# Products of probs and values issued in four runs per group of heads instead of ten

## What is computed

```python
xn = layernorm(x)                                   # x: (2, 1024, 512) float32
q, k, v = split(xn @ w_qkv.T + b_qkv)               # 32 heads of 16
scores = q @ k.T / 4 + slope[head] * (key - 1023)   # ALiBi bias, causal mask
s = (softmax(scores) @ v) @ w_out.T + b_out
g = silu(down(silu(gate(xn)) * up(xn)))             # octonion-structured, ternary weights
out = x + s * g
```

## Time and profile before

| | |
|---|---|
| Median of 3 runs | 980.35 us (979.74 to 981.66) |
| Span of the profiled execution, first to last instruction | 976.7 us |
| Median less span | 3.65 us |
| TensorE matmul busy | 920.3 us, 94% |
| VectorE busy | 648.4 us, 66% |
| ScalarE busy | 464.6 us, 48% |
| Mean granted TensorE clock | 0.978 of 2.4 GHz |
| Scores, L1257 and L1262 | 190.4 and 87.2 us of TensorE |
| Products, L1273 | 126.2 us without those that read the reused buffer |
| Maxima, L1244 and L1247 | 208.3 and 86.4 us of TensorE |

### The profile page before, as it was taken

How to read it: one execution, slowest core, us unless ns; L and a number is a source line. 1 busy time by engine, 2 the same in 40 slices (tenths; PEclk the granted TensorE clock), 3 DMA queues, 4 the chain that set the end, 5 groups by cost and what they waited for, 6 DMA issues and landing times.

```text
span 976.7 us, 17352 instructions
## 1 busy us (share of the span) xinstructions
PE 920.3 (94%) x5886; PEld 500.9 (51%) x5886; DVE 648.4 (66%) x1169; ACT 464.6 (48%) x634; POOL 109.8 (11%) x117
## 2 busy tenths in 40 slices
PE   3796999999999987999999999999999999999977
PEld 3672458546845663444444444444444444443565
DVE  5778434544454333855888878788888878883488
ACT  3573532233143211216566666666666566657610
POOL 1121203230322121210000000000000000000032
PEclk9897999999999998999999999999999999999999
DMA  7421004202400239801544676445765446743748
GB/s 202 157 82 60 1 33 154 74 1 100 145 13 11 81 131 130 99 12 44 67 75 75 87 100 89 65 71 75 100 89 75 73 72 89 100 121 109 242 155 325
DMA packets 78170, 92.36 MB, mean 95 GB/s; under 512 B 26829, under 2 KB 43213, under 8 KB 78129
## 3 DMA queue, kind: packets, MB, share of 16 engines
q1 hardware_dynamic: 78017, 91.54, 43.6%
q0 software_dynamic: 112, 0.27, 0.1%
HBM read 57.57 MB, written 33.82 MB: 94 GB/s over the span
## 4 chain that ended last, share of the span: by engine, by line
PE 52%; DMA 4%; DVE 2%; issue 2%; SPq 2%; ACT 1%; DVEq 0%; ACTq 0%
PE psum L1273 14%; PE psum L1244 14%; PE psum L1257 12%; PE psum L1247 3%; PE psum L1262 3%; DMA o_scr<-osum 2%; PE psum L248 2%; PE psum L249 2%; DMA r_scr<-den 1%; DMA probs<-in_L_attn_x 1%; PE psum L259 1%; PE psum L260 1%; DVE mx L1137 1%; SPq L1011 1%; SPq L1016 1%
## 5 line engine op out<-in xcount | busy, mean ns | idle before, releaser
L1137 DVE TENSOR_REDUCE mx<-psum 128x1 f32<-128x512 f32 (+3 forms) x608 | 372.2, 658 | 83.8 <-PE psum L1247 48.2
L1094 ACT ACTIVATE probs<-psum 128x1024 f32<-128x1024 f32 (+1 forms) x256 | 222.8, 915 | 117.6 <-PE psum L1262 97.7
L1244 PE MATMUL psum<-Ks,Qs 99*128 99x512 bf16 (+3 forms) x768 | 208.3, 329 | 7.5 <-issue 5.6
L1257 PE MATMUL psum<-Qs,Ks 102*128 102x512 bf16 (+3 forms) x768 | 190.4, 326 | 2.1 <-DVE g_stage L304 1.6
L248 PE MATMUL psum<-X,MG 128*128 128x512 f16 (+1 forms) x352 | 136.7, 388 | 5.0 <-PEq L322 3.7
L249 PE MATMUL psum<-X,MG 128*128 128x512 f16 (+1 forms) x352 | 136.4, 387 | 0.0
L1244 PEld LDWEIGHTS psum<-Ks,Qs 99*128 99x128 bf16 x768 | 65.6, 98 | 134.7 <-DVE mx L1137 76.9
L1273 PE MATMUL psum<-probs,Vs 128*32 128x512 f32 (+3 forms) x1152 | 126.2, 521 | 0.0
L1257 PEld LDWEIGHTS psum<-Qs,Ks 102*128 102x128 bf16 x768 | 72.0, 98 | 55.6 <-ACT probs L1094 8.4
L276 ACT ACTIVATE hid<-psum,sig_scale 128x512 f32<-128x512 f32 (+1 forms) x44 | 30.2, 687 | 147.5 <-PE psum L249 147.5
L1262 PE MATMUL psum<-identb,causal 128*128 128x128 bf16 (+1 forms) x384 | 87.2, 237 | 0.0
(11 more groups left out here) (124 smaller groups left out, 1093.0 us busy)
## 6 DMA issues: line engine op xcount, KB each, us to landing
Qs<-q_scr SPq DMA_DIRECT2D x96, 128.0 KB
Ks<-k_scr SPq DMA_DIRECT2D x96, 128.0 KB
o_scr<-osum SPq DMA_DIRECT2D x32, 256.0 KB, 4.1
q_scr<-qk_stage SPq DMA_DIRECT2D x16, 384.0 KB, 2.4
k_scr<-qk_stage SPq DMA_DIRECT2D x16, 384.0 KB, 2.5
v_scr<-v_stage SPq DMA_DIRECT2D x16, 256.0 KB, 2.0
g_scr<-g_stage SPq DMA_DIRECT2D x16, 256.0 KB, 2.0
Vs<-v_scr SPq DMA_DIRECT2D x16, 256.0 KB
```

What stands on the lines that cost most here:

```text
L1094: nc.scalar.activation(probs[n % PSLOTS][:, 2 * pair:2 * pair + 2, 0:COLS[n]], s_bank[pair][:, :, 0:COLS[n]], ACT.Exp, scale=1.0 / INV_SCA ...
L1137: nc.vector.tensor_reduce(dst, m_bank[bank][:, 0:n * keys].rearrange("p (n k) -> p n k", n=n), AX.X, ALU.max).then_inc(max_read, 1)
L1244: last = nc.tensor.matmul(tile[:, hh, :], Qs[s][0:ROWS_MAX, h + hh, qb * P:(qb + 1) * P], Ks[s][0:ROWS_MAX, h + hh, k0:k0 + keys], start=( ...
L1257: last = nc.tensor.matmul(bank[:, at:at + cols], Ks[s][0:ROWS_ALL, 2 * pair + h, kb * P:(kb + 1) * P], Qs[s][0:ROWS_ALL, 2 * pair + h, (c ...
```

## The change

A table RUNS says after the scores of which step which products are listed. After step 1: those of steps 7, 8 and 9 of the group before; after step 4: 0, 1 and 2; after step 6: 3 and 4; after step 8: 5 and 6. The costs that interleave gives them are the same, and so are the maxima and their pacing, the matmuls themselves, all semaphores and counts, the exps and their places on ScalarE, and SP's queue. After the last group steps 7, 8 and 9 follow as before.

```diff
--- before.py
+++ after.py
@@ -103,6 +103,7 @@
 LAST_PACE = 0.7
 LAG = 3
 PSLOTS = 5
+RUNS = {1: (-1, (7, 8, 9)), 4: (0, (0, 1, 2)), 6: (0, (3, 4)), 8: (0, (5, 6))}
 LATE = [t % SLOTS for t in (QUADS - 3, QUADS - 2)]
 
 
@@ -121,10 +122,8 @@
     main = []
     for n in range(NST):
         main += [("scores", 0, (n, pair), 2 * COLS[n] + 2 * P * len(STEPS[n][1]) * (n in DIAG)) for pair in range(2)]
-        if n >= LAG:
-            main.append(("products", 0, n - LAG, 4 * COLS[n - LAG]))
-        elif not first:
-            main.append(("products", -1, NST + n - LAG, 4 * COLS[NST + n - LAG]))
+        if n in RUNS and not (first and RUNS[n][0]):
+            main += [("products", RUNS[n][0], m, 4 * COLS[m]) for m in RUNS[n][1]]
     items = [(1, i) for i in range(LEAD, NITEM)] if ahead else []
     items += [(2, i) for i in (range(LEAD) if lead else [ROWS_AT])] if ahead else []
     cost = [PARTS_COST if i == ROWS_AT else MAXT[i - (i > ROWS_AT)][2] * MAXT[i - (i > ROWS_AT)][4] + 64 for _, i in items]
```

## The result

The changed kernel takes 1031.26 us, the median of four runs (1029.92 to 1031.76), against 980.67 us (979.74 to 981.66) of the kernel before in the same rounds: a ratio of 1.052 [1.0505, 1.0536], 5.2% slower. The forecast was 1033.7. Between the medians lie 50.6 us, where the forecast added 53.3; the two profiled executions, each one run out of several, lie 53.2 apart (spans of 1029.9 and 976.7 us).

The account below looks back on a forecast made before the run. TensorE's order was taken to price each group. Adding 1 + 46.5 + 5.8 = 53.3 us for group 0, thirteen groups and the end to 980.35 gave 1033.7 us, 5.4% slower, range 1018 to 1042.

Parts of the forecast that it names:

- Rival A: Runs behave as announced, ScalarE is not in the way and only switches go: 18 us faster, 962 us; chance 0.03.
- rival C: Stalls as forecast but the switches saved too, 2.3 us a group: 1017 us with the ends; chance 0.05.
- ScalarE's cover: Steady groups: scores following each other with only maxima between wait for ScalarE's exps, 3.58 us a group, 46.5 over thirteen.
- rival B: No change: same work, ten switches, and maxima cover ScalarE wholly; 980 us; chance 0.04.
- S2 S3 S4: Scores of steps 2 to 4, up to product 0: TensorE waits for ScalarE's exps and copy, 1.54 us lost a group.
- S5 S6: Scores of steps 5 and 6, up to product 3: TensorE waits for exps, 0.76 us lost a group.
- S7 S8: Scores of steps 7 and 8, up to product 5: TensorE waits for exps, 0.40 us lost a group.
- S9 S0 S1: Scores of steps 9, 0 and 1 over the group's border: TensorE waits for exps, 0.88 us lost a group.
- The ends: Group 0 adds 1 us (0 to 3.6); group 14 and the start of group 15 add 5.8 us.
- The last store: Kernel's end: the last osum waited 3.85 us for SP; group 15 uses 2.5 of it, still covered.
- rival D: Dearer: m5's DMA or the last store comes late on top, 1038 to 1045 us; chance 0.06.
- The switch: TensorE between full-width matmuls and 32-column products: 0.22 us both ways, made as often as before, so 0 saved.

Follow-up runs that it names:

- closed: Changed kernel with maxima kept out of the product runs and put behind them, so TensorE switches four times a group in place of ten: 1043.74 us, ratio 1.0655.
- one_run: Order of the kernel before, ten single product places, except that products 0, 1 and 2 all stand after the scores of step 4: 1003.56 us, ratio 1.0228.
- split_two: Kernel before, with only the products of steps 3 and 5 cut into halves with a maximum between, two more switches a group: 1001.80 us, ratio 1.0209.
- split: Kernel before, with the products of steps 0 and 3 to 7 cut into halves with a maximum between, six more switches a group: 1015.96 us, ratio 1.0366.

## Why the prediction was right

**The order.** The forecast said that maxima stay between the products of a run and that no switch is saved. It was right: in the trace after the change ten separate runs of products stand in a group, so the four of the title are those of the list, not of what is issued, and keeping the maxima out (the kernel with real runs) changed the time by another 12.5 us. Rival A (962) and rival C (1017) rested on adjacency and fall with it; "closed" adds that adjacency alone would not have brought the gain of A either.

**ScalarE's cover.** Shown by the pair with shorter exps: 21 us in the new order, nothing in the old one. That excludes rival B. The waits came where they were forecast, and the longest at step 4 (0.74 us where 0.9 was forecast); a small one at step 0 (0.17) was not named:

| stretch | forecast, us | measured, us |
|---|---|---|
| S2 S3 S4 | 1.54 | 1.49 (one_run: 1.50 as a period) |
| S5 S6 | 0.76 | 0.72 (0.47 + 0.25) |
| S7 S8 | 0.40 | 0.27 |
| S9 S0 S1 | 0.88 | 0.66 (0.17 + 0.14 + 0.35) |
| sum | 3.58 | 3.14 |
| period less before's | 3.58 | 3.35 (33.26 - 29.91) |

The walk priced the stretches of plain scores to 0.05 us and was too dear where masked scores and the group's border lie. Some 0.2 us of the period lie outside these stretches; I can't place them.

**The ends.** Cut at the copies of a group's second half, the 53.2 us between the two profiled executions fall into five parts. The first score came at 448.24 and comes at 449.23: 1.0 us that the change can't have made, within the scatter of that start. From there to group 0's copy (484.55, now 488.42): 2.9 us, where the forecast had 1, with a bound of 3.6 (the copy comes after step 2 of group 1, so a piece of it is group 1's). The thirteen periods from there to group 13's (873.38, now 920.76): 43.5, forecast 46.5. From there to group 14's (900.39, now 953.12): 5.3, forecast 5.8. To the end: 0.5, forecast 0. That the sum agrees to 0.1 us is luck: terms that were too large and too small cancel, single terms are up to 3 us off, and 1.0 us is scatter. Between the medians it is 50.6, 2.7 less than forecast. The largest term, the period, was priced 0.23 us too dear, 3.0 over thirteen groups. The forecast of the time also carried the 3.65 us between the median and the one profiled span before; after the change the profiled execution took 1031.72 us at a span of 1029.9, 1.8 apart. The upper end of the range adds up to 64.4 us, so about 1044.8 and not 1044.5; nothing rests on it.

**The last store.** Forecast as hidden, with 2.5 of 3.85 us of cover used. SP's queue at the end, against the earlier trace rows:

```profile
953.75 0.34 SPq L969 DMA_DIRECT2D o_scr<-osum  x1
...
963.18 0.36 SPq L969 DMA_DIRECT2D o_scr<-osum  x1
...
971.19 0.60 SPq L996 DMA_DIRECT2D den<-o_scr  x1
971.84 2.51 SPq L1015 DMA_DIRECT2D chunk_room<-o_scr  x4
974.92 0.36 SPq L969 DMA_DIRECT2D o_scr<-osum  x1
```

The store in the middle is issued 56.0 us later than before and the wait behind it ends only 52.8 later. In both traces it ends shortly after the second gate load has landed, 0.7 us after 917.60 and 1.1 us after 970.11, which fits a landing held by the loads ahead of it. The last osum comes from this copy:

```profile
974.30 0.60 ACT L1104 ACTIVATE osum<-psum 128x512 f32<-128x512 f32 x1 [1.22 <-PE psum L1272]
```

It is ready at 974.90 and the store goes out at 974.92. SP had issued the load before it by 974.35, where before the change only 0.04 us lay between the two: now SP waits for the copy, some 0.5 us. All of the 3.85 us of cover is used and a little more, so "still covered" was wrong, and the last store's half of rival D has begun. From the end of one copy to the end of the next (953.72 to 974.90) it takes 21.2 us; the forecast had 19.6, 1.6 too little. The cost is small here: the store is issued 3.73 us after the load at 971.19, before it was 3.55, and the 0.5 us of the part "to the end" is all that can belong to it.

**The switch.** 0.22 us was a little small: 0.26 from the long run (a unit 0.86 instead of 0.90, so 0.17 for leaving), 0.28 and 0.29 where switches were added. It does not enter the sum; it would have made rival A's gain 6 x 0.26 x 14 = 22 us.

## What to carry to other kernels

Work of the busiest engine that looks like one block is often the cover of another engine's turn: before bunching it, walk through what the other engines do meanwhile, with the number of buffers between them, and leave enough of the other work between two steps that wait for each other. Read the order that is issued, not the list it is made from; a pacing step between them can undo the grouping and leave only its cost. The length of a run did not decide by itself: two or three products side by side, with the maxima spread between the scores, gave 1.2% to 1.4%, while the list of four places, with two or three steps of scores in a row and too little between them, lost 5.2%.

## What was not expected of the hardware

TensorE's program may not grow at no cost inside a loop. Before, the queue of instructions moves 27 packets in the whole run and none between 560 and 846 us. With the few matmuls more of split_two it moves 54, 27 of them in that stretch; TensorE stands still once per round of three groups, 2.7 to 3.1 us at a time (570.3, 666.4, 762.1 us), and the period that holds this is 4.4 us longer. Three times the growth (split) costs about the same: 2.5 to 2.8 us a round and 59 packets. The eleven other traces all have 27. So it behaves like a step between the size before and the smaller growth, not like a price for each instruction; where the step lies was not measured, nor why the period loses more than the gap. A packet of that queue starts 0.1 to 0.6 us before the last matmul ahead of each of the six standstills. That TensorE waits for its instructions there is argued from the packets and the rhythm; the profile puts the standstill down to nothing.
